# Even and odd column planes for the images of a wavelet, attention and fusion block

## The reference, cut to what matters

```python
# per level l (64 x 64, then 32 x 32): t has 4 bands per channel
t = dwconv(haar(cur), dw_w[l])                      # 5 x 5
t = coord_gate(mix(t))
hlow = strip_pool(t, 3)                             # row sums of 7, reflected, / 7
ho = hl * hlow + (1.0 + hh) * (t - hlow)
vlow = strip_pool(ho, 2)                            # column sums of 7 / 7
vo = vl * vlow + (1.0 + vh) * (ho - vlow)
t = t * bt + vo * gm                                # then a gate per band, wscale
...
x_tag = inverse_haar(levels)                        # 128 x 128
base = dwconv(x, base_w, base_b) * base_scale       # 5 x 5
init = base + g * x_tag
sattn = rconv(concat(init.mean(1), init.max(1)), sa_w, sa_b)            # 7 x 7
gate = sigmoid(rconv(concat(init, cattn + sattn), pg_w, pg_b, groups=C))  # 7 x 7
out = init + gate * a + (1.0 - gate) * y            # a = base, y = g * x_tag
return op_w @ out + op_b
```

## Time and profile before

| | |
|---|---|
| median of three runs | 2579.34 us (2573.43 to 2582.67) |
| the profiled execution | 2568.33 us, its span 2566.5 us |
| PE, DVE, ACT, POOL busy | 88%, 59%, 46%, 17% of the span |
| mean granted TensorE clock | 0.94 of full speed |
| stages by their first instructions | gated_conv from about 320, mix0 from 793, wavelet from 1280, attention maps from 1925, fusion from 1957, mix1 from 2203 us |

### The profile page before, as it was taken

How to read it: one execution, slowest core, us unless ns; L and a number is a source line. 1 busy time by engine, 2 the same in 40 slices (tenths; PEclk the granted TensorE clock), 3 DMA queues, 4 the chain that set the end, 5 groups by cost and what they waited for, 6 DMA issues and landing times. The chain is left out here.

```text
span 2566.5 us, 61875 instructions
## 1 busy us (share of the span) xinstructions
PE 2261.6 (88%) x21290; PEld 1261.1 (49%) x21290; DVE 1521.9 (59%) x2653; ACT 1175.5 (46%) x2386; POOL 448.9 (17%) x707
## 2 busy tenths in 40 slices
PE   7679859999996999999699999999984999699997
PEld 3335517785783333333266666666651342233333
DVE  3335501111113777777578888888871555488887
ACT  4346422222222888888622222222220221388887
POOL 7610006101100000000044444444420000000000
PEclk9789859999997999999899999999996999799999
DMA  6999987787754778777486666666635999344343
GB/s 151 263 253 271 244 283 236 272 268 240 262 190 93 142 144 153 141 146 149 88 159 144 145 145 145 145 145 145 143 88 125 244 263 268 111 114 116 111 114 89
DMA packets 529401, 445.99 MB, mean 174 GB/s; under 512 B 315708, under 2 KB 444676, under 8 KB 525938
## 3 DMA queue, kind: packets, MB, share of 16 engines
q1 hardware_dynamic: 459042, 413.28, 62.6%
q0 software_dynamic: 5744, 23.34, 3.6%
q10 hardware_dynamic: 64512, 7.88, 2.3%
HBM read 259.75 MB, written 186.40 MB: 174 GB/s over the span
## 5 line engine op out<-in xcount | busy, mean ns | idle before, releaser
L602 PE MATMUL gate_ps<-gate_data,gate_wt 64*64 64x289 f32 x6144 | 389.2, 410 | 25.7 <-issue 18.9
L602 PEld LDWEIGHTS gate_ps<-gate_data,gate_wt 64*64 64x64 f32 x6144 | 306.3, 134 | 109.8 <-issue 39.4
L663 DVE TENSOR_TENSOR gate_out<-gate_gelu,gate_ps 128x578 f32<-128x578 f32 x96 | 72.2, 756 | 378.3 <-PE gate_ps L602 339.2
L951 ACT CAST mix_h<-mix_bank 96x512 f16<-96x512 f32 x512 | 267.5, 591 | 10.4 <-PE mix_bank L902 6.6
L640 ACT ACTIVATE gate_gelu<-gate_ps 128x578 f32<-128x578 f32 x96 | 62.8, 654 | 295.0 <-PE gate_ps L602 275.6
L1036 DVE TENSOR_SCALAR mix_hb<-mix_h,mix_b1q 96x1024 f16<-96x1024 f16 x256 | 122.8, 480 | 98.2 <-ACT mix_h L951 98.2
L2043 PE MATMUL fus_bank<-fus_xt,fus_taps 76*32 76x512 f32 x1344 | 156.0, 613 | 26.0 <-DMA fus_shift<-gate_shift 23.5
L902 PE MATMUL mix_bank<-mix_xq,mix_w1q 112*96 112x512 fp8e5 x512 | 143.5, 382 | 38.3 <-ACT mix_h L951 23.0
L1046 DVE CAST mix_hq<-mix_hb 96x2048 fp8e5<-96x2048 f16 x128 | 156.5, 1223 | 22.1 <-DVE mix_hb L1036 20.2
L292 DVE COPY exp_out<-exp_y 128x384 f32<-128x384 f32 x192 | 102.2, 567 | 104.8 <-PE exp_y L255 53.6
L255 PE MATMUL exp_y<-exp_win,exp_xb 48*128 48x192 f32 x1024 | 117.7, 369 | 48.8 <-DVE exp_out L292 30.0
(11 more groups left out here) (227 smaller groups left out, 4103.5 us busy)
## 6 DMA issues: line engine op xcount, KB each, us to landing
y<-exp_out SPq DMA_DIRECT2D x64, 816.0 KB, 12.1
gate_data<-y SPq DMA_DIRECT2D x24, 2176.0 KB, 18.8
g<-gate_out SPq DMA_DIRECT2D x48, 578.0 KB, 4.5
mix_sc<-g SPq DMA_DIRECT2D x31, 816.0 KB
wav_strips<-xp SPq DMA_DIRECT2D x96, 204.0 KB, 3.9
wav_halves<-xp SPq DMA_DIRECT2D x48, 340.0 KB
init<-wav_init SPq DMA_DIRECT2D x48, 268.0 KB, 2.4
fus_xt<-init SPq DMA_DIRECT2D x24, 536.0 KB
```

Source lines behind the costliest of these rows:

```text
L602: mm = pe.matmul(banks(a, v)[64 * g:64 * (g + 1), r], wt[q][64 * r:64 * (r + 1), 2 * a + g, n, :], src, start=n == 0, stop=n == 3)
L951: act.copy(h16[at.pair][:, m, h, :], bank[(2 * m + h) % len(bank)][0:HID, :]).then_inc(h16_ready, 1)
```

## The change

All images between the stages (init, base, mean, peak, the map, mixed) become even and odd column planes of 64 columns, with rows and parity on the partitions: 64 partitions hold 32 rows x 2 parities or 16-row tiles in a fixed order. Around that:

- `base_conv` reads `strips` instead of `halves`, as 3 shifts x 2 halves x 4 groups = 24 matmuls of 256 columns in tiles of 64 x 32; its weights come in the record of the front weights. `halves`, `base_raw` and their DMAs go.
- There is one double bank `full_bank` for both sets. `up` of channel n-1 now waits for `base_out` of channel n. Level 0 of `up` is 4 matmuls of 256 columns in tiles of 64 x 64. `logit` has two matmuls instead of three.
- Sums of seven: four plus four (overlapping in the middle element, with two coefficients of the matrices changed to match). The operation of L1718 goes, at both levels.
- `reflect_init` moves from ScalarE to GpSimd, as four small operations behind `build_up`.
- The fusion stage's convolutions become 2 channels x 5 shifts x 2 halves x 4 groups = 80 matmuls of 256 columns and 5 x 2 x 4 = 40 of 256 columns, all in tiles of 64 x 32 on 44 rows of data. ScalarE's queue issues half of the lines and all of the weights. The result is stored in rows of 256 floats.
- mix1's loads of `sc` become rows of 64 floats, and its projection reads even and odd columns alternately. The coordinate gates' ten jobs use four double banks, four jobs at a time in four row groups.

```diff
@@ gated_conv, TensorE
-                for j, (lvl, m, g) in enumerate(JOBS):
-                    if j > 1:
-                        pe.wait_ge(gate_ready, j - 1)
-                    for r in range(2):
-                        g1 = g if lvl == 0 else r
-                        x = pe.matmul(ps[1][j % 2][0:HID, NT * r:NT * (r + 1)],
...
+                for m in range(2):
+                    for r in range(2):
+                        for g in range(4):
+                            j = 4 * m + g
+                            if m > 0 and r == 0:
+                                pe.wait_ge(gate_ready, j - 3)
+                            x = pe.matmul(job_bank(j)[:, NT * r:NT * (r + 1)],
...
@@ token_mix
-                            sp.dma_start(sc[at.pair][0][rows, :], tokens(src, at.block, at.pair, h)).then_inc(src_in[at.pair], 16)
+                            planes = src[:, bass.ds(at.block * 4, 4), :, b0:b0 + S0].rearrange("c y e j -> c (y e) j")
+                            sp.dma_start(sc[at.pair][0][rows, :].rearrange("c (k j) -> c k j", j=S0), planes
+                                         ).then_inc(src_in[at.pair], 16)
...
-                        mm = pe.matmul(x1_bank[0:CP, :], proj[:, :], sc[at.pair][0][:, :], start=True, stop=True)
+                        mm = pe.matmul(x1_bank[0:CP, :], proj[:, :], sc[at.pair][0][:, :].rearrange(
+                            "c (y e j) -> c y j e", y=4, e=2), start=True, stop=True)
@@ wavelet, TensorE
-                    for r in range(2):
-                        pe.matmul(small_bank[u][:, Q1:Q1 + B], logit_w[u][:, 0, :], sum0[u][:, r, :], start=r == 0, stop=r == 1)
+                    pe.matmul(small_bank[u][:, Q1:Q1 + B], logit_w[u][:, 0, :], sum0[u][:, :], start=True, stop=True)
...
-                    for e in range(2):
-                        for dx in range(3):
-                            for g in range(4):
-                                x = pe.matmul(images(full_bank[u][STRIP * g:STRIP * (g + 1), :])[:, :, e::2],
-                                              base_w[u][:, e, dx, :], halves[u][:, g, :, 1 + dx:1 + dx + S0],
+                    for m in range(3):
+                        for r in range(2):
+                            rows = slice(64 * r, 64 * r + K0)
+                            for g in range(4):
+                                x = pe.matmul(full(r)[STRIP * g:STRIP * (g + 1)], base_w[u][rows, m, :],
+                                              strips[u][rows, g, :, 1 + m:1 + m + S0], start=m == 0, stop=m == 2)
...
-                    pe.wait_ge(base_ready, n + 1)
+                    pe.wait_ge(base_ready, capped(n + 2, 2 * N))
...
+                    for h in range(2):
+                        for r in range(2):
+                            to = 64 * (h ^ r)
+                            x = pe.matmul(full(r)[to:to + 64], up0[u][64 * h:64 * (h + 1), :], ct0[u][64 * h:64 * (h + 1), r],
@@ wavelet, GpSimd (new; ScalarE's two copies go)
+                def reflect_init(i, u):
+                    pool.wait_ge(added, n + 1)
...
+                    pool.tensor_tensor(side_a[:, :, :], x[:, :, 2:S0 + 2:S0 - 1], side(0), ALU.mult)
+                    pool.tensor_tensor(side_b[:, :, :], x[:, :, 3:S0 + 1:S0 - 3], side(1), ALU.mult).then_inc(sides_done, 1)
+                    pool.tensor_copy(x[:, :, 0:S0 + 4:S0 + 3], x[:, :, 3:S0 + 1:S0 - 3])
+                    pool.wait_ge(sides_done, n + 1)
+                    pool.tensor_tensor(x[:, :, 1:S0 + 3:S0 + 1], side_a[:, :, :], side_b[:, :, :], ALU.add).then_inc(edged, 1)
@@ wavelet, VectorE
-                        dve.tensor_tensor(uu[:, :, :], s4[:, :, 0:s], s2[:, :, 4:s + 4], ALU.add).then_inc(at, 1)
-                        dve.wait_ge(at, 3 * n + 3)
-                        dve.tensor_tensor(uu[:, :, :], uu[:, :, :], tt[:, :, 6:s + 6], ALU.add).then_inc(ready, 1)
+                        dve.tensor_tensor(uu[:, :, :], s4[:, :, 0:s], s4[:, :, 3:s + 3], ALU.add).then_inc(ready, 1)
@@ fusion, loads and convolutions
+        def tiles(record):
+            return bass.AP(record.tensor, record.offset, [[B * XW, KF], [TILE * ROW, 4], [1, B * XW]])
+
+        def load_lines(eng, i, u, ch):
+            c = 2 * (i * SLOTS + u) + ch
+            for r in range(2):
+                eng.dma_start(xt[u][64 * r:64 * r + KF, ch].rearrange("p g b x -> p g (b x)"),
+                              tiles(t["init"][bass.ds(c, 1), 64 * r:64 * r + 1])).then_inc(in_conv[u], 16)
...
+                        for n in range(2 * SHIFTS):
+                            ch, m = n // SHIFTS, n % SHIFTS
+                            for r in range(2):
+                                rows = slice(64 * r, 64 * r + KF)
+                                for g in range(4):
+                                    mm = pe.matmul(part(u, 0)[STRIP * g:STRIP * (g + 1), r], taps[u][rows, ch, m, :],
+                                                   xt[u][rows, ch, g, :, m:m + S0], start=n == 0, stop=n == 2 * SHIFTS - 1)
...
+                with act.Fori(0, N - 1) as i:
+                    for u in S:
+                        gates(i, u)
+                        act.wait_ge(added, i * SLOTS + u + 1)
+                        load_taps(act, i + 1, u)
+                        load_lines(act, i + 1, u, 1)
```

More of the change, by code:

```diff
@@ L33 @@
     "center": CP, "average": CP,
[L34 removed]
+    "box0": 2 * H + S1, "eye": H, "box1": H, "rows0": 16, "rows1": S1, "sides": 4,
     "ones": H,
@@ L1627, in step @@
                         low_out(*front)
-                    if done is not None:
-                        reflect_init(*done)
                     if tail is not None:
@@ L1696, in _ @@
                         build(i + 1, u)
+                        reflect_init(i, u)
+                for u in U:
+                    reflect_init(N - 1, u)
             @block.vector
@@ L1931, in _ @@
                 dve.wait_ge(map_ready, 1)
-                reflect_columns(dve, out).then_inc(padded_ready, 1)
+                for e in range(2):
+                    dve.tensor_copy(out[:, e, :, 0:2], out[:, e, :, 4 - e:2 - e:-1])
+                    x = dve.tensor_copy(out[:, e, :, S0 + 2:S0 + 4], out[:, e, :, S0 + 1 - e:S0 - 1 - e:-1])
+                x.then_inc(padded_ready, 1)
 def fusion(nc, t):
@@ L1946, in each @@
             return [k.sb(f"{name}{u}", shape) for u in S]
-        spatial = k.sb("spatial", [K3, NSTRIP, B, XP])
+        spatial = k.sb("spatial", [128, 4, B, XW])
         bias, shift = k.sb("bias", [128, C]), k.sb("shift", [128, GROUP, B])
-        xt = each("xt", [K2, NSTRIP, B, XP])
-        taps = each("taps", [K2P, TAPS, STRIP])
-        halves, whole = each("halves", [K3P, 2, THIRDS, STRIP]), each("whole", [K3, THIRDS, STRIP])
-        base, init = each("base", [128, 2 * B, W]), each("init", [128, 2 * B, XP])
@@ L1954, in fusion @@
-        gate, diff, out = (each(n, [128, 2 * B, W]) for n in ("gate", "diff", "out"))
-        bank = [[k.ps(f"bank{u}{j}") for j in range(2)] for u in S]
+        xt = each("xt", [128, 2, 4, B, XW])
+        taps, whole = each("taps", [128, 4, SHIFTS, STRIP]), each("whole", [128, SHIFTS, STRIP])
+        base, init = each("base", [128, 2, 2 * Q]), each("init", [128, 2, 2 * B, XW])
+        gate, diff, out = (each(n, [128, 2, 2 * Q]) for n in ("gate", "diff", "out"))
+        bank = [k.ps(f"bank{u}", (128, 2 * NT)) for u in S]
@@ L1961, in fusion, with part @@
+        def part(u, j):
+            return bank[u][:, :].rearrange("p (r n) -> p r n", r=2)[:, :, Q * j:Q * (j + 1)]
         with nc.Block() as block:
@@ L2038, in _ @@
                         c = i * SLOTS + u
[L2039 removed]
+                        pe.wait_ge(in_conv[u], 96 * i + 96)
                         pe.wait_ge(gated, c + 1)
[L2041 to L2046 removed]
@@ L2047, in _ @@
-                        pe.wait_ge(added, c + 1)
-                        for n in range(THIRDS):
-                            for s in range(NSTRIP):
-                                mm = pe.matmul(bank[u][1][STRIP * s:STRIP * (s + 1), :], whole[u][:, n, :],
-                                               spatial[:, s, :, THIRDS * n:THIRDS * n + W],
-                                               start=n == 0, stop=n == THIRDS - 1)
-                                if n == THIRDS - 1:
-                                    mm.then_inc(map_done, 1)
+                        pe.sem_inc(pe_turn, 1)
@@ new lines, in _ @@
+                        mm.then_inc(own_done, 1)
+                        pe.wait_ge(added, c + 1)
+                        pe.sem_inc(pe_turn, 1)
+                        for m in range(SHIFTS):
+                            for r in range(2):
+                                rows = slice(64 * r, 64 * r + KF)
+                                for g in range(4):
+                                    mm = pe.matmul(part(u, 1)[STRIP * g:STRIP * (g + 1), r], whole[u][rows, m, :],
```

(5 more changed lines are left out.)

371 lines of the change are left out of this document (184 added, 187 removed).

## The result

The changed kernel takes 2615.45 us (median of four runs, 2610.89 to 2619.38) against 2576.39 for the kernel before (four runs, 2569.86 to 2582.67). The ratio is 1.0131, interval 1.0097 to 1.0164: 1.3% slower. The forecast was 2512, 2458 to 2558, with 0.05 for slower. The profiled execution of the changed kernel took 2610.89 us, its span 2609.1.

The account below looks back on a forecast made before the run. TensorE was taken to bound the wavelet stage, DMAs fusion, and the projection to be on mix1's chain. Profiled 2568.3 - 75 (wavelet) - 8 (gates) + 16 (fusion) = 2501, said as a 2512 us median; range 2458 to 2558.

Parts of the forecast that it names:

- Fusion, TensorE's part: Fusion: 160 + 80 records at 29.1 ns, 7.0 us a channel against 8.47, so TensorE does not set the pace.
- rival 3: mix1's projection: reading at stride 256 bytes adds 1.7 us in each of 64 steps, +109 us, 2621; chance 0.05.
- Fusion, the DMAs: Fusion: 7.3% more bytes at the same rate, period from 9.70 to 10.41 us over 22 channels or so, +16 us.
- Rival 1: Fusion: if pieces of 512 bytes held the DMAs, it gains, -40 instead of +16 us, 2456; chance 0.13.
- Rival 2: Fusion: loads of 44 partitions use 11 of 16 DMA engines, period 12.2 us, +55 us, 2553; chance 0.22.
- Wavelet: Wavelet stage: step from 12.94 to 11.34 us, 1.60 less in 47 steps, 75 us gained; bounds 35 and 90.
- the new wait: Wavelet: `up` of channel n-1 waits for `base_out` of channel n, 0.25 us a step; bounds 0 and 0.6.
- rival 4: Wavelet: VectorE and GpSimd hinder each other, step 12.2 us, 35 us gained instead of 75, 2552; chance 0.13.
- The main sum: Whole kernel: 2568.3 - 75 - 8 + 16 = 2501 us profiled, with mix1's strided projection read taken as 0.
- Gates: Coordinate gates: ten jobs from 24.6 to 16.7 us, 8 us less, on the path; bounds 3 and 12.

Follow-up runs that it names:

- e6_rows48: Changed kernel with 48 partitions instead of 44 in fusion's loads and matmuls, four added rows with zero weights: 2558.0 us, period 10.93.
- e2_heat: Changed kernel with 20 matmuls of 128 x 128 x 512 ahead of fusion's loop and two more before each channel's small matmuls: 2564.3 us.
- e12_rows64_alone: Changed kernel with fusion's matmuls on 64 rows instead of 44, added rows zero, cleared slot by slot: 2536.39 us, ratio 0.9836 to the kernel before.
- e15_unrolled: e12_rows64_alone with TensorE's part of fusion's loop written out for all 24 channels: 2524.2 us in one run, stage 244.2.
- experiment 3: Changed kernel, mix1's projection reading side by side, ScalarE's base_out ahead of its DMA issues: wavelet 534.4 against 537.4 us, mix1 326.1 against 337.9.

## Why the prediction was wrong, by its steps

**Fusion, TensorE's part: the step that failed.** It took 29.1 ns a record from `band_conv_0`, so 7.0 us for a channel, and said "It does not set the pace". That rate belongs to 2.4 GHz, and nothing in the argument asked whether the new stream would be granted it. Measured: 53.3 ns and 12.80 us at 1.2 GHz, and this set the pace. The rows to ask it of stood in the trace of before: in fusion the old matmuls, with 76 and 114 rows, ran at 0.50 from 1975 to 1990 though TensorE was busy 4.9 to 5.0 of every 5 us, and the clock rose only some 17 us in (0.78 in 1990 to 1995). `band_conv_0` has its rate with 48 rows, with which e6_rows48 reached 1.00 too, and amid operations on 112 and 128. The Trainium skill, "TensorE: Matmul & The Clock Gate", in "The HAM clock gate", has the clock go by how busy the engine has been; here TensorE was busy in 307 of 322 us, in the first 51 without a gap, and stayed at half. The measurement decides: rows count too.

At 2.4 GHz the same 240 records of 44 rows take 6.7 us (e2_heat), so the rate was right for that clock, and what failed is the clock that it took for granted. The 0.05 for slower lay on rival 3; that it came out slower came from a place that no rival named.

Of the 103 us that fusion grew (223.9 to 327.3) the runs part off 68 for the rows (e12_rows64_alone, 259.3), 15 for TensorE's loop (e15_unrolled, 244.2), and 20 that are left.

**Fusion, the DMAs.** The forecast was a period of 10.41 us and +16. At the full clock the period was 10.67, and 9.93 without the jump back. The period looks nearly right, but the stage does not: the kernel before gave its results every 8.80 us, not 9.70, as it lived on the lead of its first slots, and its 223.9 us became 259.3, +35 and not +16 (+20 without the jump back). The reason was right only in part: bytes have a share in the period (9.75 with 21% fewer), but so have the instructions of TensorE's loop, of which the prediction said nothing. What the 20 us that are left consist of stays open: in e15_unrolled TensorE still waits 55 us in the stage for nothing that the trace names, and no run tells apart data that are late and instructions that are late. Rival 1 (fusion gains) failed even so. Rival 2 had forecast a period of 12.2 us, near the 12.80 that came, but at a DMA share of 0.8 to 0.9 where 0.63 was measured; that nearness is luck. (By its own terms its time is 2551, not 2553.)

**Wavelet: the time right, by two errors that cancelled.** One step of the changed kernel (timeline):

```profile
1563.12 1.16 PE L1551 MATMUL wav_full_bank<-wav_ct,wav_up 128*128 128x128 f32 x8
1564.20 0.66 PE L1556 MATMUL wav_full_bank<-wav_ct,wav_up 64*64 64x256 f32 x8
1564.80 0.49 PE L1502 MATMUL wav_small_bank<-wav_t,wav_pool 128*128 128x128 f32 x2
...
1569.39 0.28 PE L1526 MATMUL wav_small_bank<-wav_sum,wav_logit_w 128*128 128x4 f32 x2
...
1569.83 1.54 PE L1540 MATMUL wav_full_bank<-wav_strips,wav_base_w 48*32 48x256 f32 x48
1571.50 0.70 PE L1474 MATMUL wav_small_bank<-wav_strips,wav_front_w 112*32 112x128 f32 x16
1572.13 2.40 PE L1483 MATMUL wav_front<-wav_strips,wav_front_w 48*32 48x256 f32 x80
1574.46 1.16 PE L1551 MATMUL wav_full_bank<-wav_ct,wav_up 128*128 128x128 f32 x8
```

From `up` to `up` 11.34 us, as forecast; level 0 of `up` 0.60 (0.60), logits 0.44, 0.22 less (0.19). But the base convolution takes 1.67 from start to start, not 1.40, and the matmuls of `up` don't have the new wait: 2.33 from `band_conv_0` to `up`, as in the earlier trace rows (only weight loads waited for `base_out`, experiment 3). In its place TensorE waits 0.17 us for ct ahead of the low band in every other step (21 times in 500 us), presumably because the shorter base convolution no longer covers squash and weighing; no run tests that. Two errors of a quarter of a microsecond cancelled. The mean step is 537.4 / 47 = 11.43, the stage 70 us shorter against 75. VectorE was no bound (403 of 500 us), rival 4 did not come.

**mix1: right mechanism in rival 3, wrong size in both places.** The main sum had 0, rival 3 1.7 us a step; measured 0.22 at most, 11 to 12 us in all. The low band, which reads every other column, was no guide to a distance of 64.

**Gates.** 8 us forecast, 8.5 at the place, 0 to 4 at the wavelet stage.

By the profiled executions: 2501 forecast, 2610.9 measured. Fusion 87 over its +16, mix1 11, wavelet 5, gates 4 to 8, together 107 to 111 of the 110 between them.

## What to carry to other kernels

Before a rate is taken over from one matmul to another, look at the granted clock of the stretch it will stand in, and at how many rows the rate had: a stage of matmuls alone, busy without a gap, can still stand at half clock, and filling the rows (with zeros, if need be) cost next to nothing here and gave back 68 us. Count a loop's instructions as well as its bytes when it is split into more, smaller matmuls. Where an engine stands at the point where its loop jumps back, the arrow in the trace can name an engine that had long been done.

## What the runs showed of the hardware that I had not expected

- The granted clock by rows, TensorE otherwise busy: 44 rows in tiles of 64 x 32: 0.50 for 322 us, and when it started at 1.00, 0.50 to the end of the stage from the first stand of 2.48 us on; 48 and 64 rows: down behind stands, and back to 1.00; 68 rows in tiles of 128 x 32: 0.50 for 400 us, where 76 and 114 rows had 1.00.
- A float32 matmul of 512 columns that reads elements 256 bytes apart: 760 ns for 654 in the median; writing every other column of a bank costs nothing (654).
- A stand of 4.05 us of TensorE was followed by 4 us at a granted clock of 0.57.
- GpSimd's copy of 640 columns on 44 partitions to another half of the partitions took 0.71 us; it freed 110 KB of DMA a channel.
